# A scan over 25 chunks of nodes: passes ordered step by step, own rows added in PSUM, and the DMA transpose used from pass 12 on

## The chip, the core and the metric

The kernel runs on one core of a Trainium2 chip. The metric is the device time of one execution in microseconds (us). Three runs of the kernel before took 3808.49, 3808.58 and 3815.07 us; the median is 3808.58.

## The reference

Inputs are node features x (6250 nodes, 256 channels) and 206,250 edges sorted by destination. What is computed, cut to what matters:

```python
# 1. graph attention over layernorm(x)
h = (layernorm(x) @ W).reshape(n, 4, 64)
e = leaky_relu(a_src[src] + a_dst[dst], 0.2)
alpha = softmax of e over the edges of each destination
x = x + relu(segment_sum(alpha * h[src], dst) + bias)
# 2. a scan of 30 steps over layernorm(x), row by row
def step(h, _):
    h = h + 0.01 * tanh(h)
    h = h * sigmoid(h)
    h = layernorm(h) * ln_w + ln_b
    return einsum('bsc,dc->bsd', h, W) + b
x = x + scan(step, layernorm(x), length=30)
```

In the scan no row depends on another row, but each of a row's 30 steps depends on the one before it.

## The kernel before

**Tiles and chunks.** The nodes lie in 49 tiles of 128 rows x 256 channels, one row of each tile per partition. For the scan two tiles make a chunk (`CH = 2`), which gives `NC = 25` chunks; the last, chunk 24, has one tile. A *pass* is one scan step of one chunk, so there are 30 x 25 = 750 passes (`ALL`), numbered in the order of the list `ORDER`.

**Attention first.** Up to about 2200 us the core gathers edge rows and forms sums by destination. The scan's function `scan_ffn` then finishes the attention per tile: it fetches a tile's sum row (`end_row`, an indirect DMA from GpSimd), weights it (`gathered`, VectorE, `scale`), weights the tile's own row, the self loop (`own_tile`, four ScalarE instructions a tile, one for each head, `own`), adds the two (`own_added`, VectorE, `add`), adds the result to X behind a relu (`added`, VectorE, `both`), and takes the layernorm statistics (`spread`, `means`, `roots`) and the normalised rows (`normalise`, ScalarE, `ready`). For the first 14 tiles (7 chunks) this is done at once, the adding on TensorE (`add_own`). The other 35 tiles come in five batches of seven, and their pieces are laid between the passes: `PLANS` gives for each batch and stage the step at which it starts and every how many steps a tile follows. `due(q, stage)` says which piece stands at step q.

**One pass.** Each engine has its own instruction stream, written out step by step by a function `step(p)`. For pass q:

1. ScalarE `tanh(q)`: waits for the `affine` of the same chunk's previous pass (`act.wait_ge(s_aff, ...)`, line 1389).
2. GpSimd `add(q)`: h + tanh(h), line 1286.
3. ScalarE `silu(q)`, line 1369.
4. VectorE `stats(q)` (two instructions, one for each tile) and `moments(q)`; it waits for `silu(q)`, line 1579.
5. The transpose, in one of two ways. *Near*: four TensorE transposes into PSUM (`transposes`) and a ScalarE copy back (`copy_t`). *Far*: ScalarE splits each 32-bit word into two 16-bit halves (`split`, line 1381), SyncE sends them to DRAM (`send`, line 1216) and a transposing DMA brings them back (`turn`, line 1223). `FAR[q]` says which.
6. TensorE `product(q)`: four 32-bit products of 128x128 with 128x256, which the profile counts as eight matmuls, line 1682.
7. GpSimd `root(q)`: 1/sqrt of the variance; from `FAR0` on one instruction for three passes.
8. VectorE `affine(q)`: scales the product by the root and adds the bias, one instruction for each tile, line 1600. It frees the chunk for its next pass.

**The order of the steps.** Within step p ScalarE does `tanh(p)`, then `split(p-2)` if that pass is far, then `silu(p-1)`, then `copy_t(p-3)`. VectorE runs ahead (`AHEAD = 3`) and its affine behind (`BEHIND = 2`):

```python
lead = p.on(AHEAD)
lag = p if p.n < FAR0 else p.on(-BEHIND)
if leads: stats(lead)
if lags:  affine(lag, 0)
if leads: moments(lead)
if lags:  affine(lag, 1)
```

TensorE does `transposes(p)`, then `product(p-2)` before FAR0 and `product(p-4)` after it. SyncE does `send(p)`, then `turn(p-2)`. All streams are in order.

**Which chunks are in turn.** `ORDER` runs chunks 0 to 6 twelve times (84 passes, all near, `FAR0 = 84`), then chunks 0 to 9 eighteen times, chunks 10 to 16 and 7 to 9 twelve times, chunks 10 to 24 eighteen times, and chunks 17 to 24 twelve times. From pass 84 on chunks 0, 3, 6, ... are near and the others far: 432 passes of 750. Seventeen turns of the 15 chunks stand in a hardware loop on every engine (`iterate`); the rest is straight code.

Of the kernel before, what the change touches and what calls it, by code (L numbers as in the profile page):

```python
# [51 lines left out]
QT = 7  # L52
# [12 lines left out]
U = 5  # L65
assert NC % U == 0 and CH == 2 and SHORT == 1
# [8 lines left out]
assert len(ORDER) == ALL and len(LATER) % U == 0  # L75


FAR0 = JOIN * LAG
TURN = len(LATER)
RT, RX, RV, G3 = 3, 5, TURN, 3  # L80
assert TURN % RT == 0 and TURN % RX == 0 and TURN % G3 == 0 and FAR0 % G3 == 0 and ALL % G3 == 0
NEAR_J = [j for j in range(NC) if j % 3 == 0]
assert NC - 1 in NEAR_J
FAR = [q >= FAR0 and j not in NEAR_J for q, j in enumerate(ORDER)]
# [16 lines left out]
PASS = [q + 1 for q in range(ALL)]  # L101
# [5 lines left out]
XB = [0, 1, 2, 0, 1]  # L107
BANKED = []
for q in range(ALL):
    same = [p for p in range(max(q - 2 * TURN, 0), q) if not FAR[p] and XB[p % RX] == XB[q % RX]]  # L110
    BANKED.append(NEARS[same[-1]] if same else 0)

TOGETHER = ORDER.index(NC - 1) + 1
LOOPS = ITERS - LAG - 1
OUT = [0, JOIN, NA, NB, 20, 23, NC]
APART = TOGETHER + LOOPS * len(LATER)
assert all(ORDER[q] == LATER[(q - TOGETHER) % len(LATER)] for q in range(TOGETHER - len(LATER), APART))

SEEN = {}
FORMER = []  # L120
for q, j in enumerate(ORDER):
    FORMER.append(SEEN.get(j))
    SEEN[j] = q


FT = [0, 4, 8, 14, 21, 28, 35, 42, NT]
NF = len(FT) - 1
FRONT = 3
assert FT[FRONT] == CH * JOIN
OWN_ACT = [2, 2, 3]  # L130
assert all(b - a == QT for a, b in zip(FT[FRONT:], FT[FRONT + 1:]))


class Plan:


    def __init__(self, fetch, pace, below, share, norm, scale, own, add, step, mean, root, ready, every):
        n = QT
        self.at = dict(fetch=(fetch, pace, n), below=(below, 1, 1), share=(share, 1, 1), norm=(norm, 1, 1),
                       scale=(scale, step, n), own=(own, step, n), add=(add, step, n), both=(add + 1, step, n),  # L140
                       spread=(add + 2, step, n), mean=(mean, 1, 1), root=(root, 1, 1), ready=(ready, every, n))


AHEAD, BEHIND = 3, 2
DONE = {q0 + 3 * (j - j0) + BEHIND: j for j0, j1, q0 in ((0, JOIN, SEEN[0] + 5), (JOIN, NA, SEEN[JOIN] + 5), (NA, NB, APART + 2))
        for j in range(j0, j1)}
DONE.update({SEEN[j] + 2 + BEHIND: j for j in range(NB, NC)})


PLANS = {FRONT: Plan(5, 3, 25, 33, 34, 35, 42, 43, 4, 70, 77, 80, 2)}  # L150
for b in range(FRONT + 1, NF):
# [4 lines left out]
def due(q, stage):  # L156

    if q.r is not None:
        return None
    for b, plan in PLANS.items():  # L160
        first, every, count = plan.at[stage]
        i = q.n - first
        if 0 <= i < every * count and i % every == 0:
            return b, i // every
    return None
HS = 100.0


class At:


    def __init__(self, n, r=None):
        self.n, self.r, self.j, self.w = n, r, None, 0
        if 0 <= n < ALL:
            self.j = ORDER[n]
            self.w = SHORT if self.j == NC - 1 else CH
            self.u, self.v, self.t = n % RX, n % RV, n % RT
            self.far = FAR[n]

    def on(self, d):  # L180
        return At(self.n + d, self.r)

    def runs(self):
        return 0 <= self.n < ALL

    def of(self, table, less=0, times=1):

        n, rise = self.n, 0
        if self.r is not None:
            rise = table[n + TURN] - table[n]  # L190
            assert all(table[n + k * TURN] == table[n] + k * rise for k in range(LOOPS))
        first = times * (table[n] - less)
        return first if self.r is None or not rise else self.r * (times * rise) + first
# [936 lines left out]
def scan_ffn(nc, sem, res, dram, out, s_merged):  # L1130
# [3 lines left out]
    with ExitStack() as ctx:  # L1134
# [20 lines left out]
        assert U == 5 and FT[1] * C == 2 * 512 == (FT[2] - FT[1]) * C and (FT[3] - FT[2]) * C == 3 * 512  # L1155
# [9 lines left out]
        s_ownt = sem("s_ownt")  # L1165
        s_taken = sem("s_taken")
# [28 lines left out]
        def iterate(eng, step, after):  # L1195

            for q in range(TOGETHER):
                step(At(q))
            with eng.Fori(0, LOOPS) as r:
                for n in range(TOGETHER, TOGETHER + TURN):  # L1200
                    step(At(n, r))
            for q in range(APART, ALL + after):
                step(At(q))

        def sync(sp):
# [5 lines left out]
            def send(q):  # L1211
                sp.wait_ge(s_split, q.of(FARS))
                sp.nop(nofuse=True)
                wait_count(sp, s_turned[q.u], q.of(TURNED, 1, 16))
                sp.nop(nofuse=True)
                sp.dma_start(turned[q.u, :, :], hs[:, q.t, :].bitcast(U16)).then_inc(s_sent[q.t], 16)

            def turn(q):
                sp.wait_ge(s_sent[q.t], q.of(SENT, 0, 16))
                sp.nop(nofuse=True)  # L1220
                wait_count(sp, s_prod, q.of(PASS, RX))
                sp.nop(nofuse=True)
                sp.dma_start_transpose(h2T[:, q.u, :].bitcast(U16).rearrange("p (b n) -> p b n", n=2 * P),
                                       turned[q.u, :, :].rearrange("p (l c) -> (p l) c", l=2)).then_inc(s_turned[q.u], 16)
# [3 lines left out]
            def store(j0, j1):  # L1228
                sp.wait_ge(s_fin, j1)
# [9 lines left out]
            loads = {PLANS[b - 2].at["add"][0] + PLANS[b - 2].at["add"][1] * (QT - 1) + 4: b for b in range(FRONT + 2, NF)}  # L1239
            stores = {max(d for d, j in DONE.items() if j0 <= j < j1) + 4: (j0, j1) for j0, j1 in zip(OUT, OUT[1:])}  # L1240

            def step(p):
                if p.r is None and p.n in loads:
                    b = loads[p.n]
                    sp.wait_ge(s_taken, b - FRONT - 1)
                    own_rows(b)
                if p.r is None and p.n in stores:
                    store(*stores[p.n])
                if p.runs() and p.far:
# [5 lines left out]
            iterate(sp, step, 2 + 10)  # L1255
            assert max(stores) < ALL + 12
            sp.wait_ge(s_out, 16 * parts[0])

        def gpsimd(pool):
# [20 lines left out]

            def add(q):
                pool.wait_ge(s_tanh, q.of(PASS))
                wait_count(pool, s_silu, q.of(PASS, RT))
# [4 lines left out]
            def root(q, count):  # L1288
                last = q.on(count - 1)
                pool.wait_ge(s_ve, last.of(PASS))  # L1290
                wait_count(pool, s_aff, last.of(PASS, RV))
# [17 lines left out]
            def step(p):  # L1309
                if p.r is None and p.n < 5:  # L1310
# [5 lines left out]
                if p.runs():  # L1316
                    add(p)
                q = p.on(-3)
# [5 lines left out]
            iterate(pool, step, 3)  # L1324

        def scalar(act):
# [57 lines left out]
            def tanh(q):  # L1384
# [3 lines left out]
                else:  # L1388
                    act.wait_ge(s_aff, q.of(PASS, q.n - FORMER[q.n]))
                wait_count(act, s_add, q.of(PASS, RT))  # L1390
# [26 lines left out]
            def step(p):  # L1417
                if p.r is None and p.n < 5:
# [310 lines left out]
```

## Time and profile before

| | |
|---|---|
| median of 3 runs | 3808.58 us |
| profiled execution | 3808.91 us |
| its span, first to last instruction | 3807.1 us |
| TensorE, VectorE, ScalarE, GpSimd busy | 1542.5, 3081.4, 2453.4, 2987.5 us |
| GpSimd adds of the scan (line 1286) | 750, 941.0 us |
| product matmuls (line 1682) | 5880, 1348.1 us |
| transposing DMAs (line 1223) | 432, median 3.3 us from issue to landing |

The page gives busy times over the whole span, and in the slices of the span each digit is the busy share of one fortieth (95 us) in tenths. Since the attention stage fills more than half of the span, what the change touches has to be read in stretches behind 2237 us. Where instructions of an engine overlap (a ScalarE instruction of 0.62 us is followed after 0.52), the distance from start to start says what one costs, and not its duration.

### The profile page before, as it was taken

The page shows a single profiled execution, that of the slowest core. Times are in us where ns is not written, and L with a number is a line of the kernel's source. Part 1 is how long each engine was busy: PE and PEld are TensorE (multiplying, and loading weights), DVE is VectorE, ACT ScalarE, POOL GpSimd, SP SyncE. Part 2 cuts the span into 40 slices and gives each one's busy share as a digit, 9 for nine tenths or more (in the row PEclk, how much of TensorE's full clock was granted, in tenths as well). Part 3 has the DMA queues.
Part 4 walks back from the last instruction along what each step waited for, and adds up shares of the span by engine and source line. Part 5 has one row for each costly group of instructions (what it writes and reads, how often), then busy time and mean ns, then how long its engine had stood idle before and what let it go on. Part 6 is the DMA issues. An engine that isn't in the chain of part 4 may idle for free.

```text
span 3807.1 us, 42139 instructions
## 1 busy us (share of the span) xinstructions
PE 1542.5 (41%) x7470; PEld 1310.1 (34%) x7470; DVE 3081.4 (81%) x7292; ACT 2453.4 (64%) x3821; POOL 2987.5 (78%) x2856
## 2 busy tenths in 40 slices
PE   2400000000000000000000059999998999999988
PEld 2300000000000000000000048877876788888866
DVE  7477777877777878777877858989998988888877
ACT  4344444444444444444444557899999999999976
POOL 6777777777777777777777659988887889999876
PEclk8755555555555555555555569999999999999999
DMA  7366666666666666666666620266667777787766
GB/s 202 130 201 219 215 213 212 220 220 220 219 215 213 213 218 212 225 215 213 214 219 219 229 86 13 56 164 157 165 162 177 182 189 194 194 193 194 178 163 157
DMA packets 631730, 713.59 MB, mean 187 GB/s; under 512 B 499785, under 2 KB 501866, under 8 KB 615269
## 3 DMA queue, kind: packets, MB, share of 16 engines
q1 hardware_dynamic: 546180, 480.32, 42.4%
q0 software_dynamic: 83824, 230.16, 20.6%
q10 hardware_dynamic: 1536, 1.18, 0.2%
q14 instruction: 145, 1.19, 0.1%
q8 instruction: 45, 0.74, 0.1%
HBM read 249.79 MB, written 349.24 MB: 157 GB/s over the span
## 4 chain that ended last, share of the span: by engine, by line
POOL 40%; PE 21%; issue 19%; DMA 7%; ACT 6%; DVE 4%; SPq 0%; ACTq 0%; DVEq 0%; POOLq 0%
POOL G L737 36%; PE ps L1682 18%; DMA G<-haug,idx 3%; DMA h2T<-turned 3%; POOL h L1286 3%; ACT hs L1381 2%; PE ps L1668 2%; ACT h L1369 1%; ACT th L1392 1%; DVE cst L1582 1%; DVE Hs L1600 1%; POOL rs L1293 1%; PE psum L1016 1%; ACT own L1338 1%; DVE cmv L1591 1%
## 5 line engine op out<-in xcount | busy, mean ns | idle before, releaser
L737 POOL DMA_INDIRECT G<-haug,idx x1612 | 1524.4, 946 | 497.5 <-issue 482.8
L1682 PE MATMUL ps<-WT,h2T 128*128 128x256 f32 x5880 | 1348.1, 383 | 64.1 <-DMA h2T<-turned 61.7
L1682 PEld LDWEIGHTS ps<-WT,h2T 128*128 128x128 f32 x5880 | 1096.9, 191 | 226.4 <-DMA h2T<-turned 84.6
L1286 POOL TENSOR_TENSOR h<-Hs,th 128x512 f32<-128x512 f32 x750 | 941.0, 1265 | 188.5 <-ACT th L1392 179.5
L973 DVE TENSOR_TENSOR_SCAN RS<-keep,psum 128x845 f32<-128x845 f32 x496 | 940.2, 1898 | 0.2
L1058 PE MATMUL psum<-AD,ones 128*128 128x512 f32 x2 | 2.1, 1142 | 2052.5 <-DVE AD L1075 2052.5
L1600 DVE SCALAR_TENSOR_TENSOR Hs<-ps,rs,b 128x256 f32<-128x256 f32 x1470 | 675.4, 460 | 153.8 <-PE ps L1682 136.2
L644 ACT ACTIVATE G<-RS 128x845 f32<-128x845 f32 x496 | 782.2, 1723 | 26.6 <-DVE RS L973 25.5
L636 ACT ACTIVATE decay<-el,ZC 128x4 f32<-128x4 f32 x124 | 37.1, 299 | 1045.1 <-DVE el L943 1045.1
L1058 PEld LDWEIGHTS psum<-AD,ones 128*128 128x128 f32 x2 | 0.5, 310 | 2052.8 <-DVE AD L1075 2052.8
L1582 DVE BATCH_NORM_STATS2 cst<-h 128x6 f32<-128x256 f32 x1470 | 547.7, 413 | 51.9 <-ACT h L1369 49.7
L1369 ACT ACTIVATE h<-h 128x512 f32<-128x512 f32 x750 | 459.2, 612 | 65.6 <-POOL h L1286 62.6
L1392 ACT ACTIVATE th<-Hs 128x512 f32<-128x512 f32 x750 | 458.0, 611 | 42.9 <-DVE Hs L1600 38.7
L954 DVE TENSOR_TENSOR psum<-G,psum 128x845 f32<-128x845 f32 x496 | 477.5, 1031 | 2.4 <-ACT psum L637 2.4
L1381 ACT ACTIVATE hs<-h 128x1024 uint16<-128x1024 uint16 x432 | 451.2, 1044 | 10.2 <-DMA turned<-hs 10.2
L1293 POOL TENSOR_TENSOR rs<-cmv,half_neg 128x6 f32<-128x6 f32 (+1 forms) x306 | 360.0, 1177 | 26.9 <-DVE cmv L1591 25.7
L912 DVE TENSOR_TENSOR z<-G,AD 128x52 f32<-128x52 f32 x124 | 30.4, 245 | 410.6 <-DMA G<-haug,idx 358.6
L1668 PE MATMUL ps<-ident,h 128*128 128x128 f32 x1212 | 191.6, 280 | 41.0 <-ACT h L1369 38.9
L1591 DVE BATCH_NORM_AGGREGATE cmv<-cst 128x2 f32<-128x9 f32 x1470 | 188.9, 169 | 1.2
L1375 ACT ACTIVATE h2T<-ps 128x512 f32<-128x512 f32 (+1 forms) x318 | 177.4, 559 | 10.9 <-PE ps L1668 10.9
L1668 PEld LDWEIGHTS ps<-ident,h 128*128 128x128 f32 x1212 | 151.3, 144 | 89.7 <-ACT h L1369 54.7
L963 DVE SCALAR_TENSOR_TENSOR psum<-RS,decay,psum 128x65 f32<-128x65 f32 x492 | 124.6, 322 | 0.6 <-DVE z L912 0.4
(161 smaller groups left out, 1175.5 us busy)
## 6 DMA issues: line engine op xcount, KB each, us to landing
sums<-G SPq DMA_DIRECT2D x124, 1716.0 KB, 6.6
turned<-hs SPq DMA_DIRECT2D x432, 256.0 KB, 2.4
G<-haug,idx POOLq DMA_INDIRECT x1612, 2.8
h2T<-turned SPq DMA_TRANSPOSE x432, 3.3
haug<-G SPq DMA_DIRECT2D x7, 924.0 KB, 3.7
X<-x SPq DMA_DIRECT2D x7, 784.0 KB, 21.6
own<-haug SPq DMA_DIRECT2D x5, 924.0 KB, 4.8
adz<-G SPq DMA_DIRECT2D x4, 830.5 KB, 32.3
```

The costliest lines, as they stand in the source:

```text
L644: last = nc.scalar.activation(G[:, k % R, :, h * HR:(h + 1) * HR].rearrange("p t f -> p f t"), RS[:, k % 2, h, :, :], ACT.Copy)
L737: pool.indirect_dma_start(out=G[:, u, t, :], out_offset=None, in_=haug[:, :], in_offset=bass.IndirectOffsetOnAxis(ap=idx[:, i % 2, u * T + ...
L954: last = v.tensor_tensor(ps_m[:, h, :, :].rearrange("p f t -> p t f"), G[:, u, :, h * HR:(h + 1) * HR], w, ALU.mult)
L973: v.tensor_tensor_scan(RS[:, k % 2, h, :, :].rearrange("p f t -> p (f t)"), keep[:, k % 2, :, :].rearrange("p f t -> p (f t)"), ps_m[:, h, ...
L1286: g.tensor_tensor(h1[:, q.t, 0:n], chunk_rows(Hs, q.j, q.w), th[:, q.t, 0:n], ALU.add).then_inc(s_add, 1)
L1369: nc.scalar.activation(h2[:, q.u, 0:n], h1[:, q.t, 0:n], ACT.Silu, scale=1.0 / HS).then_inc(s_silu, 1)
L1381: nc.scalar.activation(hs[:, q.t, :].bitcast(U16).rearrange("p (l c) -> p l c", l=2), h2[:, q.u, :].bitcast(U16).rearrange("p (c l) -> p l ...
L1392: nc.scalar.activation(th[:, q.t, 0:n], chunk_rows(Hs, q.j, q.w), ACT.Tanh, scale=1.0 / HS).then_inc(s_tanh, 1)
L1582: last = v.bn_stats(cst[:, q.v, a, 0:6], h2[:, q.u, a * C:(a + 1) * C])
L1600: ins = v.scalar_tensor_tensor(out=Hs[:, q.j * CH + a, :], in0=ps_g[q.u][:, a * C:(a + 1) * C], scalar=rs[:, q.v, a:a + 1], in1=b100[:, :] ...
L1668: last = nc.tensor.transpose(ps_x[XB[q.u]][:, n * P:(n + 1) * P], h2[:, q.u, n * P:(n + 1) * P], ident[:, :])
L1682: last = nc.tensor.matmul(ps_g[q.u][:, a * C:(a + 1) * C], h2T[:, q.u, (a * 2 + k) * P:(a * 2 + k + 1) * P], WT[:, k, :], start=(k == 0), ...
```

## The change

Four things change together.

1. **The order of the passes.** `ORDER` is made by a rule: at each step, of the chunks that are ready and were last passed at least 7 (before step 94) or 10 steps ago, the one with most passes left is taken; chunks 0 to 9 count as if they had 8 fewer left. The batches follow each other every 80 steps instead of every 67. The hardware loop is gone, all 750 passes are straight code, and the `nop` instructions between SyncE's waits are dropped.
2. **Own rows.** `own_tile` moves from ScalarE (four instructions a tile) to GpSimd (one). The VectorE add of own rows goes; TensorE adds both rows in a PSUM bank (`add_tile`), from which VectorE's `added` reads. The near transposes keep two PSUM banks instead of three.
3. **Far passes** begin with pass 12 (`FAR0 = 12`) and are those with q % 3 != 2, except of chunk 24.
4. **SyncE** issues `turn` one step behind `send` and no longer two.

The steps of ScalarE and of VectorE within a pass, `AHEAD` and `BEHIND` stay. Chunks are stored in eight groups (`OUT`).

```diff
-LAG = 12
-JOIN, NA, NB = 7, 10, 17
-LATER = list(range(NA, NC))
-ORDER = (list(range(JOIN)) * LAG + list(range(NA)) * (ITERS - LAG) + (list(range(NA, NB)) + list(range(JOIN, NA))) * LAG
-         + LATER * (ITERS - LAG) + list(range(NB, NC)) * LAG)
-FAR0 = JOIN * LAG
-NEAR_J = [j for j in range(NC) if j % 3 == 0]
-FAR = [q >= FAR0 and j not in NEAR_J for q, j in enumerate(ORDER)]
...
-PLANS = {FRONT: Plan(5, 3, 25, 33, 34, 35, 42, 43, 4, 70, 77, 80, 2)}
+PLANS = {FRONT: Plan(5, 3, 25, 33, 34, 35, 41, 43, 43, 4, 70, 77, 80, 2)}
 for b in range(FRONT + 1, NF):
-    q = 24 + 67 * (b - FRONT - 1)
-    PLANS[b] = Plan(q, 8, q + 54, q + 62, q + 63, q + 64, q + 71, q + 72, 9, q + 130, q + 138, q + 141, 3)
+    q = 24 + 80 * (b - FRONT - 1)
+    PLANS[b] = Plan(q, 8, q + 54, q + 62, q + 63, q + 64, q + 70, q + 72, q + 72, 11, q + 141, q + 148, q + 151, 3)
...
+def ready_at(j):
+    t = min(CH * j + CH, NT) - 1
+    if t < FT[FRONT]:
+        return 0
+    b = (t - FT[FRONT]) // QT + FRONT
+    first, every, _ = PLANS[b].at["ready"]
+    return first + every * (t - FT[b]) + 1
+
+ALL = ITERS * NC
+FAR0, EARLY = 12, 94
+APART, WIDE = JOIN, 10
+FAVOUR = 8
+
+def passes():
+    left, last, made = [ITERS] * NC, [-ALL] * NC, []
+    for q in range(ALL):
+        apart = APART if q < EARLY else WIDE
+        free = [j for j in range(NC) if left[j] and ready_at(j) <= q and q - last[j] >= apart]
+        j = max(free, key=lambda j: (left[j] - FAVOUR * (j < WIDE), -last[j], -j))
+        made.append(j)
+        left[j] -= 1
+        last[j] = q
+    return made
+
+ORDER = passes()
+FAR = [q >= FAR0 and q % 3 != 2 and j != NC - 1 for q, j in enumerate(ORDER)]
+DONE = {q + BEHIND + 2: j for j, q in SEEN.items()}
+OUT = [(10, 14), (14, 17), (17, 21), (21, NC), (0, 4), (4, 7), (7, 9), (9, 10)]
...
-        ps_x = [psum[:, n * 512:(n + 1) * 512] for n in (4, 5, 6)]
+        ps_x = [psum[:, n * 512:(n + 1) * 512] for n in (4, 5)]
+        ps_m = psum[:, 6 * 512:6 * 512 + C]
...
-        def iterate(eng, step, after):
-            for q in range(TOGETHER):
-                step(At(q))
-            with eng.Fori(0, LOOPS) as r:
-                for n in range(TOGETHER, TOGETHER + TURN):
-                    step(At(n, r))
-            for q in range(APART, ALL + after):
-                step(At(q))
+        def iterate(step, after):
+            for q in range(ALL + after):
+                step(At(q))
...
 SyncE:
-            loads = {PLANS[b - 2].at["add"][0] + PLANS[b - 2].at["add"][1] * (QT - 1) + 4: b for b in range(FRONT + 2, NF)}
+            loads = {PLANS[b - 2].last("add") + 2: b for b in range(FRONT + 2, NF)}
+            stores = {max(SEEN[j] for j in range(j0, j1)) + BEHIND + 6: (j0, j1) for j0, j1 in OUT}
-                q = p.on(-2)
-                if q.runs() and q.far:
+                q = p.on(-1)
+                if q.runs and q.far:
                     turn(q)
...
 GpSimd:
+            def own_tile(b, i):
+                if i == 0:
+                    pool.wait_ge(s_own[b], 16)
+                    pool.wait_ge(s_part, b + 1)
+                o = own[:, b % 2, i, 0:SUMS].rearrange("p (h f) -> p h f", h=H)[:, :, 0:HID]
+                g.tensor_tensor(o, o, part[:, b % 2, 1, i, :].unsqueeze(2).to_broadcast([P, H, HID]), ALU.mult).then_inc(s_ownt, 1)
...
 ScalarE:
-                if due(p, "own"):
-                    own_tile(*due(p, "own")).then_inc(s_ownt, 1)
...
 VectorE:
-            def own_added(b, i0, i1):
-                hs = tile_heads(Hs[:, FT[b] + i0:FT[b] + i1, :], HID)
-                return v.tensor_tensor(hs, hs, tile_heads(own[:, b % 2, i0:i1, :], HR), ALU.add)
...
+                    gathered(b, i, i + 1).then_inc(s_weighted, 1)
                 if due(q, "both"):
                     b, i = due(q, "both")
+                    n = tiles_before(b) + i
+                    dve.wait_ge(s_joined, n + 1)
+                    added(b, i, i + 1, ps_m).then_inc(s_taken, 1)
...
 TensorE:
+            def add_tile(b, i):
+                n = tiles_before(b) + i
+                pe.wait_ge(s_weighted, n + 1)
+                pe.wait_ge(s_ownt, n + 1)
+                wait_count(pe, s_taken, n)
+                to = heads(ps_m, HID)
+                nc.tensor.matmul(to, ident[:, :], heads(Hs[:, FT[b] + i, :], HID), start=True, stop=False)
+                nc.tensor.matmul(to, ident[:, :], heads(own[:, b % 2, i, :], HR), start=False, stop=True).then_inc(s_joined, 1)
...
             def step(p):
+                if due(p, "add"):
+                    add_tile(*due(p, "add"))
                 if 4 <= p.n < ALL and not p.far:
                     transposes(p)
```

## Rows read from the trace of the kernel before

**Rows 1.** The page, busy tenths in 40 slices of the span

```profile
PE   2400000000000000000000059999998999999988
...
PEclk8755555555555555555555569999999999999999
```

**Rows 2.** Stretches, GpSimd's line 1286 alone: bounds, length, busy (count), clock, DMA share, GB/s

```profile
2279.00:2439.70 160.70, 92.01 (x72) 1.00 0.06 17
2463.20:2799.00 335.80, 198.45 (x156) 0.98 0.66 160
3017.60:3098.00 80.40, 50.92 (x40) 1.00 0.74 181
3632.80:3662.20 29.40, 12.20 (x10) 0.88 0.73 166
3683.40:3786.30 102.90, 58.60 (x49) 0.98 0.66 156
```

**Rows 3.** Stretches: PE, PEld, DVE, ACT, POOL busy (count), clock, DMA share, GB/s

```profile
2463.00:2862.20 399.20, 370.96 (x1789) 313.43 (x1789) 364.88 (x1230) 373.11 (x659) 343.02 (x274) 0.99 0.67 161
3158.40:3428.60 270.20, 270.20 (x1342) 237.67 (x1341) 241.19 (x870) 269.31 (x450) 247.13 (x201) 1.00 0.79 194
```

**Rows 4.** Timeline of TensorE in the hardware loop: start, length, instruction

```profile
3190.44 0.60 PE L1668 MATMUL ps<-ident,h 128*128 128x128 f32 x4
3190.87 5.35 PE L1682 MATMUL ps<-WT,h2T 128*128 128x256 f32 x24
```

**Rows 5.** Timeline of ScalarE in the hardware loop

```profile
3185.01 1.04 ACT L1381 ACTIVATE hs<-h 128x1024 uint16<-128x1024 uint16 x1
3185.96 0.61 ACT L1369 ACTIVATE h<-h 128x512 f32<-128x512 f32 x1
3186.48 0.57 ACT L1375 ACTIVATE h2T<-ps 128x512 f32<-128x512 f32 x1
3186.95 0.62 ACT L1392 ACTIVATE th<-Hs 128x512 f32<-128x512 f32 x1
```

**Rows 6.** Groups by line from 2463 to 2862 us: count, busy, mean ns, idle before

```profile
L1338 ACT ACTIVATE own<-own,partw 128x64 f32<-128x64 f32 x80 | 21.1, 339 | 0.0
...
L1493 DVE SCALAR_TENSOR_TENSOR X<-Hs,X 128x256 f32<-128x256 f32 x19 | 15.2, 803 | 0.0
L1489 DVE TENSOR_TENSOR Hs<-Hs,own 128x256 f32<-128x256 f32 x19 | 14.8, 781 | 0.0
...
L1345 ACT ACTIVATE Hs<-X,nmr,rstd 128x256 f32<-128x256 f32 x14 | 8.3, 591 | 0.0
...
L1369 ACT ACT_TABLE_LOAD x2 | 2.6, 1283 | 0.0
```

**Rows 7.** Timeline of ScalarE and VectorE in the stretch with 8 chunks

```profile
3708.75 0.61 ACT L1369 ACTIVATE h<-h 128x512 f32<-128x512 f32 x1
...
3709.39 0.75 DVE L1582 BATCH_NORM_STATS2 cst<-h 128x6 f32<-128x256 f32 x2 [0.27 <-ACT h L1369]
...
3710.06 0.47 DVE L1600 SCALAR_TENSOR_TENSOR Hs<-ps,rs,b 128x256 f32<-128x256 f32 x1
...
3711.18 0.63 ACT L1392 ACTIVATE th<-Hs 128x512 f32<-128x512 f32 x1 [0.51 <-DVE Hs L1600]
...
3711.72 1.04 ACT L1381 ACTIVATE hs<-h 128x1024 uint16<-128x1024 uint16 x1
...
3712.66 0.62 ACT L1369 ACTIVATE h<-h 128x512 f32<-128x512 f32 x1
```

**Rows 8.** Groups by line and shape in the hardware loop, 3158.4 to 3428.6 us

```profile
L1286 POOL TENSOR_TENSOR h<-Hs,th 128x256 f32<-128x256 f32 x10 | 7.3, 732 | 0.0
```

**Rows 9.** Waits, whole span: who waited for whom, total us, times, longest

```profile
PEld ps L1682 <- DMA h2T<-turned: 84.6, 81, 9.1
```

**Rows 10.** A stretch at half clock, all engines

```profile
2263.00:2273.00 10.00, 7.05 (x23) 5.46 (x24) 5.85 (x21) 6.95 (x13) 9.47 (x10) 0.50 0.10 27
```

**Rows 11.** Timeline of TensorE in that stretch

```profile
2269.06 3.62 PE L1682 MATMUL ps<-WT,h2T 128*128 128x256 f32 x8
2272.47 0.74 PE L1668 MATMUL ps<-ident,h 128*128 128x128 f32 x3
```

More of the change, by code:

```diff
@@ L82, with __init__, last @@
-NEAR_J = [j for j in range(NC) if j % 3 == 0]
-assert NC - 1 in NEAR_J
-FAR = [q >= FAR0 and j not in NEAR_J for q, j in enumerate(ORDER)]
+assert CH == 2 and SHORT == 1
+FT = [0, 4, 8, 14, 21, 28, 35, 42, NT]
+NF = len(FT) - 1
+FRONT = 3
+JOIN = FT[FRONT] // CH
+assert FT[FRONT] == CH * JOIN
+OWN_ACT = [2, 2, 3]
+assert all(b - a == QT for a, b in zip(FT[FRONT:], FT[FRONT + 1:]))
+HS = 100.0
+class Plan:
+    def __init__(self, fetch, pace, below, share, norm, scale, own, add, both, step, mean, root, ready, every):
+        n = QT
+        self.at = dict(fetch=(fetch, pace, n), below=(below, 1, 1), share=(share, 1, 1), norm=(norm, 1, 1),
+                       scale=(scale, step, n), own=(own, step, n), add=(add, step, n), both=(both, step, n),
+                       spread=(both + 1, step, n), mean=(mean, 1, 1), root=(root, 1, 1), ready=(ready, every, n))
+    def last(self, stage):
+        first, every, count = self.at[stage]
+        return first + every * (count - 1)
@@ new lines, with due @@
+PLANS = {FRONT: Plan(5, 3, 25, 33, 34, 35, 41, 43, 43, 4, 70, 77, 80, 2)}
+for b in range(FRONT + 1, NF):
+    q = 24 + 80 * (b - FRONT - 1)
+    PLANS[b] = Plan(q, 8, q + 54, q + 62, q + 63, q + 64, q + 70, q + 72, q + 72, 11, q + 141, q + 148, q + 151, 3)
+def due(q, stage):
+    for b, plan in PLANS.items():
+        first, every, count = plan.at[stage]
+        i = q.n - first
+        if 0 <= i < every * count and i % every == 0:
+            return b, i // every
+    return None
+def ready_at(j):
[5 more added lines that the diff above has]
+    return first + every * (t - FT[b]) + 1
@@ L87, in tally @@
+FORMER = []
+for q, j in enumerate(ORDER):
+    FORMER.append(SEEN.get(j))
+    SEEN[j] = q
+RT, RX, RV, G3 = 3, 5, 15, 3
+assert RV % G3 == 0 and FAR0 % G3 == 0 and ALL % G3 == 0
+FAR = [q >= FAR0 and q % 3 != 2 and j != NC - 1 for q, j in enumerate(ORDER)]
 def tally(marks):
@@ L98, in ring_tally @@
     return of
-PASS = [q + 1 for q in range(ALL)]
 NEARS = tally(not f for f in FAR)
@@ L106 @@
 ROOTS = [q + 1 if q < FAR0 else FAR0 + (q - FAR0) // G3 + 1 for q in range(ALL)]
[L107 to L141, printed above, removed]
@@ L166, with __init__ @@
-HS = 100.0
-class At:
[L172 to L175, printed above, removed]
+AHEAD, BEHIND = 3, 2
+DONE = {q + BEHIND + 2: j for j, q in SEEN.items()}
+FINISHED = {DONE[d]: n + 1 for n, d in enumerate(sorted(DONE))}
+OUT = [(10, 14), (14, 17), (17, 21), (21, NC), (0, 4), (4, 7), (7, 9), (9, 10)]
+assert sorted(j for a, b in OUT for j in range(a, b)) == list(range(NC))
+class At:
+    def __init__(self, n):
+        self.n = n
+        self.runs = 0 <= n < ALL
+        if self.runs:
+            self.j, self.far = ORDER[n], FAR[n]
@@ L176, in __init__ @@
             self.w = SHORT if self.j == NC - 1 else CH
-            self.u, self.v, self.t = n % RX, n % RV, n % RT
-            self.far = FAR[n]
+            self.u, self.v, self.t, self.x = n % RX, n % RV, n % RT, NEARS[n] % 2
     def on(self, d):
[L181 to L193, printed above, removed]
+        return At(self.n + d)
@@ L1228, in store @@
             def store(j0, j1):
-                sp.wait_ge(s_fin, j1)
+                sp.wait_ge(s_fin, max(FINISHED[j] for j in range(j0, j1)))
                 for p0, p1, t0, t1, rows in node_rows(out, j0 * CH, min(j1 * CH, NT)):
@@ L1238, in sync @@
                 own_rows(b)
-            loads = {PLANS[b - 2].at["add"][0] + PLANS[b - 2].at["add"][1] * (QT - 1) + 4: b for b in range(FRONT + 2, NF)}
-            stores = {max(d for d, j in DONE.items() if j0 <= j < j1) + 4: (j0, j1) for j0, j1 in zip(OUT, OUT[1:])}
+            loads = {PLANS[b - 2].last("add") + 2: b for b in range(FRONT + 2, NF)}
+            stores = {max(SEEN[j] for j in range(j0, j1)) + BEHIND + 6: (j0, j1) for j0, j1 in OUT}
+            assert len(stores) == len(OUT)
             def step(p):
-                if p.r is None and p.n in loads:
+                if p.n in loads:
                     b = loads[p.n]
-                    sp.wait_ge(s_taken, b - FRONT - 1)
+                    sp.wait_ge(s_joined, tiles_before(b - 1))
                     own_rows(b)
-                if p.r is None and p.n in stores:
+                if p.n in stores:
                     store(*stores[p.n])
-                if p.runs() and p.far:
+                if p.runs and p.far:
                     send(p)
-                q = p.on(-2)
-                if q.runs() and q.far:
+                q = p.on(-1)
+                if q.runs and q.far:
                     turn(q)
-            iterate(sp, step, 2 + 10)
-            assert max(stores) < ALL + 12
+            iterate(step, BEHIND + 7)
             sp.wait_ge(s_out, 16 * parts[0])
@@ L1288, in root @@
             def root(q, count):
[L1289 to L1291 removed]
+                last = q.n + count - 1
+                pool.wait_ge(s_ve, last + 1)
+                wait_count(pool, s_aff, last + 1 - RV)
                 of = slice(q.v, q.v + count)
@@ L1309, in step @@
             def step(p):
-                if p.r is None and p.n < 5:
+                if p.n < 5:
                     return
@@ L1315, in step @@
                     roots(due(p, "root")[0])
-                if p.runs():
+                if p.runs:
                     add(p)
+                if due(p, "own"):
+                    own_tile(*due(p, "own"))
                 q = p.on(-3)
@@ L1322, in step @@
                     root(q.on(1 - G3), G3)
-            iterate(pool, step, 3)
+            iterate(step, 3)
         def scalar(act):
@@ L1417, in step @@
             def step(p):
-                if p.r is None and p.n < 5:
+                if p.n < 5:
                     return
@@ L1421, in step @@
                     shares(due(p, "share")[0])
-                if due(p, "own"):
-                    own_tile(*due(p, "own")).then_inc(s_ownt, 1)
                 if due(p, "ready"):
                     normalise(*due(p, "ready"))
-                if p.runs():
+                if p.runs:
                     tanh(p)
                 q = p.on(-2)
-                if q.runs() and q.far:
+                if q.runs and q.far:
                     split(q)
                 q = p.on(-1)
-                if q.runs():
+                if q.runs:
                     silu(q)
@@ L1436, in step @@
                     copy_t(q)
-            iterate(act, step, 3)
+            iterate(step, 3)
         def vector(dve):
@@ L1642, in step @@
                     affine(lag, 1)
-                if p.r is None and p.n in DONE:
+                if p.n in DONE:
                     final(DONE[p.n])
-            iterate(dve, step, BEHIND + 2)
+            iterate(step, BEHIND + 2)
         def tensor(pe):
@@ L1704, in step @@
                     product(p.on(-4))
-            iterate(pe, step, 4)
+            iterate(step, 4)
         return sync, gpsimd, scalar, vector, tensor
```

134 lines of the change are left out of this document (45 added, 89 removed).

## The prediction, made before the kernel was run

> **What bounds the kernel now.** The page's slices come first: up to the 23rd an attention stage runs, in which TensorE is nearly idle and which the change does not touch. From 2237 us on the scan runs: 750 passes (30 steps of 25 chunks), each with one GpSimd add, so the adds counted in a stretch give its pace [rows 1, 2]. I divide: 160.7/72 = 2.23 us a pass in the start phase (7 chunks in turn, all transposed on TensorE), 335.8/156 = 2.15 with 10 chunks in turn, 80.4/40 = 2.01 where these have hardly any work beside them, 102.9/49 = 2.10 with the last 8. The hardware loop, 15 chunks in turn, took 270.2 us for 150 passes (GpSimd's 201 are 150 adds, 50 roots and one that reaches in): 1.80 [rows 3].
>
> What a pass takes of an engine is the distance from one start to the next. TensorE: 0.43 for four transposes [rows 4]; its loop turn is 27.02 us with 4.5 chunks transposed and 14.5 multiplied, so a product takes (27.02 - 1.94)/14.5 = 1.73. ScalarE: split 0.95, silu 0.52, copy 0.47, tanh 0.52 like silu [rows 5]. The loop is TensorE's: busy 270.2 of 270.2 [rows 3]. With 10 chunks nobody is full: TensorE needs 1.73 + 0.4 x 0.43 = 1.90 a pass; ScalarE 1.04 + 0.6 x 0.95 + 0.4 x 0.47 + (21.1 + 8.3 + 2 x 2.6)/187 = 1.98, the bracket being own rows, normalising and two kinds of table loads, one of them shown [rows 6]; VectorE 364.9/187 = 1.95; GpSimd 343.0/187 = 1.83 [rows 3]. The 2.15 lies 0.17 over the largest; the 2.01 lies 0.15 over 1.73 + 0.3 x 0.43 = 1.86.
>
> **The order written out by hand.** What each stage waits for is in the code, its price in the trace. VectorE's step p is stats(p+3), then affine(p) before FAR0 and affine(p-2) from FAR0 on. ScalarE's step p is tanh(p), split(p-2), silu(p-1), copy. tanh(p) waits for the affine of its chunk's previous pass, with 7 chunks affine(p-7). Before, this stood in VectorE's step p-7, behind stats(p-4): slack of three steps. Now FAR0 goes from 84 to 12 while the chunks in turn stay 7, so affine(p-7) stands in step p-5, **behind stats(p-2)**, which waits for silu(p-2), which ScalarE issues in step p-1, the last thing of weight ahead of tanh(p). So silu(p-2), stats(p-2), affine(p-7), tanh(p), split(p-2), silu(p-1) is a closed ring that holds one pass; nothing overlaps round it. The last stretch of before, with 8 chunks, has the same ring with two passes in it and shows the links: silu starts at 3708.75, stats 3709.39, affine (two halves) 3710.06, tanh 3711.18, split 3711.72, the next silu 3712.66 [rows 7]. Once round is 3.91 us, and 0.94 less, 2.97, for a pass without a split. Two of three passes are split: (2 x 3.91 + 2.97)/3 = 3.60 a pass. With 8 chunks the ring allows 1.95, under the 2.10 measured; there the way through the DMAs, 8 x 2.10 = 16.8 us, decides.
>
> **The change part by part.** The new order, worked out from the rule in the diff, has distance 7 for passes 19 to 82 and once at 90, and 10 or more from 94 on; 472 passes are split (432 before), 278 transposed on TensorE.
> - Passes 0 to 11: unchanged, pass 12 starts at 2279.0 [rows 2].
> - Passes 12 to 18 and 83 to 93: 18 at the 2.23 of before or a little more, 2.3: 41.
> - Passes 19 to 82: 64 x 3.60 = 230, plus 3 for one exp table change (1.28 there and 1.28 back [rows 6]), which stands in the ring: 233. They took 143. VectorE's tile pieces (the longest 0.80 [rows 6]) fit its idle part of a round, 3.60 less the 1.79 from stats to tanh [rows 7], and GpSimd's new work fits too: nothing. If that cover failed, 7 tiles with three pieces of at most 0.80 would be 17.
> - Passes 94 to 433: own rows leave ScalarE (0.26 x 80 = 21.1 of 187 passes) and the own add leaves VectorE (14.8) [rows 6]. GpSimd gets 7 multiplies in 80 passes: 0.73 each as its 128x256 add [rows 8], at most the 1.27 of a 128x512 one. TensorE gets two matmuls a tile: half a product, 0.86. Tile work comes every 80 passes, not every 67. Per pass: TensorE 1.73 + 0.14 + 0.08 = 1.95; ScalarE 1.04 + 0.63 + 0.16 + 0.08 = 1.91; GpSimd 1.83 + 0.06 = 1.89 (1.94 with 1.27); VectorE 1.95 - 0.11 = 1.84. add_tile puts three waits on TensorE, and transposes and products, and behind these the affines, queue behind them; but the weighting is 8 steps earlier, the own multiply 2, the previous tile's taking 11: none is last. On this floor comes 0 to 0.17, as before. SyncE issues the transposing DMA one step, some 2 us, earlier, and waits for it were in the list [rows 9], so I take 0.10: 340 x 2.05 = 697.
> - Passes 434 to 679: no tile work, one short chunk in 10, 3.4 transposed: (9.5 x 1.73 + 3.4 x 0.43)/10 = 1.79. The hardware loop is gone and the distance is 10, not 15; that costs 0 to 0.15 (the 2.01 stretch, straight code with 10 chunks). Between the two, 0.08: 246 x 1.87 = 460.
> - Passes 680 to 749: floor 1.84, plus 0.10: 136. The store of 14 tiles made 10 passes last 29.4 us, 8.4 over 21.0 [rows 2]; 22 tiles leave between steps 684 and 695 and 7 at 732, by size 17; the longer distance covers a part: 14. Sum 150.
> - At nothing: SyncE's dropped nops; the third PSUM bank for transposes (two now hold six passes' worth); the fetches of own rows, still three later ones; the 25 closing adds on VectorE, at two tiles each about 25 x 1.6 = 40 us in 70 passes at the most, which fill VectorE without passing TensorE's 1.84 by more than the 0.10 taken.
> - Tail: 3807.1 - 3786.3 = 20.8. 20 tiles instead of 15 are stored after the last turn, 0.66 MB at the stretch's 156 GB/s [rows 2], 4 us, half of it under the last products: 23.
>
> Sum: 2279 + 41 + 233 + 697 + 460 + 150 + 23 = 3883 of span. The profiled execution took 1.8 more than its span (3808.9 to 3807.1; the median is 3808.6): **3885 us**, 2.0% slower. Up to pass 84 the sum gives 251 us where 161 stood; from there to the last add 1330 where 1347 stood.
>
> A rule of the Trainium skill (TensorE: Matmul & The Clock Gate, Part 1) speaks further against the change: half clock is the resting state, and only activity releases it. The trace agrees: with TensorE busy 7.05 of 10 us the granted clock was 0.50, its lower level [rows 10].
>
> **Rivals.**
> 1. The ring does not close, and the 7 chunks are held only by the way through the DMAs: 16.8 less the one step of 2.1 is 14.7, over 7 is 2.10, so 64 x 1.50 = 96 less: 3789, faster. For: rows 7 show a round with time to spare, and no stretch of before has a ring of one pass. Against: each link is a step of an in-order engine or a semaphore in the code. It decides if passes 19 to 82 run under 2.3. 10%.
> 2. The ring at half clock: a product then took 2272.47 - 2269.06 = 3.41 [rows 11], a third of the transposes twice 0.14 more: 3.70 a pass, over the 3.60, so TensorE becomes the bound: 64 x 0.10 = 6 more, 3891. For: TensorE would be busy 1.87 of 3.60, less than in rows 10. Against: the gaps are short, and over the start phase the clock held 1.00 [rows 2]. 15%.
> 3. The ring as priced, the later passes at their floors, the stores free: 34 + 20 + 14 less, 3817. Against: no straight stretch of before stood at its floor. 10%.
> 4. The ring, and later passes with the old excess: 340 x 0.07 + 246 x 0.07 = 41 more, 3926. For: the distance stays 10 to the end. 15%.
>
> **How the numbers follow.** The forecast (3850 to 3910) has 50%. Only rival 1 is faster; this kernel's measurement tells 0.2%, 7.6 us, from no change. Faster 0.09, within 0.03, slower 0.88. The range leaves out rival 1 and part of 3: 3830 to 3930.
>
> **What would show it.** Right: adds of passes 19 to 82 about 3.6 us apart, there VectorE idle ahead of stats with silu as the releaser and ScalarE idle ahead of tanh with affine as the releaser, once a pass; 2.05 for passes 94 to 433, 1.87 for 434 to 679; own multiplies near 0.73. Wrong: a start phase that stays at some 2.2 us a pass.

## The result, and the profile after

The changed kernel took 3859.67 us (median of 4 runs, 3855.04 to 3863.41). Its ratio to the kernel before, from the means of four runs each, is 1.0129, 95% interval [1.0111, 1.0147]: slower, as forecast, by 1.3% where 2.0% was said, and inside the range. The profiled execution took 3855.04 us with a span of 3853.2.

The page of the changed kernel, as in [rows 1]; the scan's first slices, the 24th to 26th, are where TensorE is less busy than behind and its clock low:

```profile
PE   2400000000000000000000066789999999999998
...
PEclk8755555555555555555555578899999999999999
```

The stretches of the changed kernel by the adds of its passes (now line 1288), as in [rows 2]: passes 19 to 83, 94 to 433, 434 to 679, 680 to 748. A count one above the passes is an add that reaches in.

```profile
2295.50:2538.00 242.50, 82.42 (x66) 0.82 0.42 103
...
2564.10:3244.30 680.20, 432.21 (x341) 1.00 0.77 183
3244.40:3687.30 442.90, 297.86 (x246) 1.00 0.71 176
3687.40:3830.90 143.50, 86.14 (x70) 0.98 0.74 181
```

242.5/65 = 3.73 us a pass in the start phase, which was 2.23 [rows 2]; 680.2/340 = 2.00 where 2.15 stood for the first 156 of these passes and 2.11 for all 340 (716.7 us from add to add); 442.9/246 = 1.80, as in the old hardware loop [rows 3], which was 1.84 over the same 246 passes (452.8 us); 143.5/69 = 2.08. Pass 94 starts 101 us later than before, and the way from there to the last add is 56 us shorter: 1266.9 where it was 1323.4.

The same stretches with all instructions of the changed kernel, columns as in [rows 3]:

```profile
2295.50:2538.00 242.50, 166.35 (x630) 136.09 (x629) 119.25 (x430) 130.00 (x202) 125.90 (x106) 0.82 0.42 103
...
2564.10:3244.30 680.20, 669.53 (x3284) 578.94 (x3283) 609.20 (x2187) 651.77 (x1057) 621.47 (x511) 1.00 0.77 183
```

In the start phase VectorE, ScalarE and GpSimd are busy about half of the time, TensorE 69% of it at a lowered clock, and nothing is full; in passes 94 to 433 TensorE nearly is, 669.5 of 680.2, with ScalarE close behind, 651.8. The waits of the start phase (2295 to 2538 us: who waited for whom, total us, times, longest) are near-equal, about one each per pass, which is how a closed ring looks:

```profile
POOL h L1288 <- ACT th L1396: 116.1, 61, 4.1
DVE cst L1555 <- ACT h L1373: 115.0, 64, 3.8
ACT th L1396 <- DVE Hs L1573: 114.4, 63, 2.8
...
DVE Hs L1573 <- PE ps L1663: 8.8, 15, 0.9
```

One round of it in the timeline, the same links as [rows 7], but now with every pass in its own round:

```profile
2357.36 0.62 ACT L1373 ACTIVATE h<-h 128x512 f32<-128x512 f32 x1
...
2358.00 0.75 DVE L1555 BATCH_NORM_STATS2 cst<-h 128x6 f32<-128x256 f32 x2 [2.25 <-ACT h L1373]
...
2358.67 0.47 DVE L1573 SCALAR_TENSOR_TENSOR Hs<-ps,rs,b 128x256 f32<-128x256 f32 x1
...
2359.78 0.63 ACT L1396 ACTIVATE th<-Hs 128x512 f32<-128x512 f32 x1 [1.33 <-DVE Hs L1573]
...
2360.32 1.04 ACT L1385 ACTIVATE hs<-h 128x1024 uint16<-128x1024 uint16 x1
...
2361.27 0.61 ACT L1373 ACTIVATE h<-h 128x512 f32<-128x512 f32 x1
```

From silu to silu 3.91 us, to the hundredth what rows 7 gave; VectorE idles 2.25 of it waiting for silu, ScalarE 1.33 waiting for affine.

### The profile page after: what moved, and what is told of

The parts are those of the page before. It is cut to its first block, busy times and chain, and to the rows that moved or that the text cites. A ratio compares the mean times of both kernels' runs of the same rounds, so it can differ in the third digit from the quotient of the medians.

```text
span 3853.2 us, 38727 instructions
## 1 busy us (share of the span) xinstructions
PE 1571.7 (41%) x7450; PEld 1341.9 (35%) x7450; DVE 3035.4 (79%) x7257; ACT 2435.4 (63%) x3681; POOL 2988.6 (78%) x2843
## 4 chain that ended last, share of the span: by engine, by line
POOL 38%; PE 22%; issue 18%; DMA 9%; ACT 5%; DVE 4%; SPq 2%; ACTq 0%; DVEq 0%; POOLq 0%
POOL G L732 36%; PE ps L1663 18%; DMA turned<-hs 4%; DMA G<-haug,idx 3%; ACT hs L1385 2%; PE ps L1649 2%; DMA h2T<-turned 2%; SPq L1216 2%; POOL h L1288 2%; ACT h L1373 1%; DVE Hs L1573 1%; ACT th L1396 1%; PE psum L1011 1%; DVE cst L1555 1%; DVE cmv L1564 1%
## 5 line engine op out<-in xcount | busy, mean ns | idle before, releaser
L1663 PE MATMUL ps<-WT,h2T 128*128 128x256 f32 x5880 | 1365.9, 387 | 25.6 <-DMA h2T<-turned 24.2
L1663 PEld LDWEIGHTS ps<-WT,h2T 128*128 128x128 f32 x5880 | 1118.0, 195 | 190.8 <-DMA h2T<-turned 44.7
L1288 POOL TENSOR_TENSOR h<-Hs,th 128x512 f32<-128x512 f32 (+1 forms) x750 | 936.9, 1260 | 250.6 <-ACT th L1396 245.3
L1555 DVE BATCH_NORM_STATS2 cst<-h 128x6 f32<-128x256 f32 x1470 | 547.7, 413 | 156.4 <-ACT h L1373 155.2
L1396 ACT ACTIVATE th<-Hs 128x512 f32<-128x512 f32 (+1 forms) x750 | 458.5, 612 | 116.9 <-DVE Hs L1573 116.9
L1385 ACT ACTIVATE hs<-h 128x1024 uint16<-128x1024 uint16 x472 | 493.7, 1046 | 17.9 <-DMA turned<-hs 17.1
L1373 ACT ACTIVATE h<-h 128x512 f32<-128x512 f32 (+1 forms) x750 | 458.6, 611 | 45.4 <-POOL h L1288 44.9
L1295 POOL TENSOR_TENSOR rs<-cmv,half_neg 128x6 f32<-128x6 f32 (+1 forms) x258 | 339.9, 1318 | 13.7 <-DVE cmv L1564 12.8
L1649 PE MATMUL ps<-ident,h 128*128 128x128 f32 x1052 | 171.3, 286 | 96.7 <-ACT h L1373 95.8
L1649 PEld LDWEIGHTS ps<-ident,h 128*128 128x128 f32 x1052 | 135.4, 147 | 136.1 <-ACT h L1373 104.6
L1379 ACT ACTIVATE h2T<-ps 128x512 f32<-128x512 f32 (+1 forms) x278 | 154.7, 557 | 13.6 <-PE ps L1649 13.5
```

The costliest lines, as they stand in the source:

```text
L1288: g.tensor_tensor(h1[:, q.t, 0:n], chunk_rows(Hs, q.j, q.w), th[:, q.t, 0:n], ALU.add).then_inc(s_add, 1)
L1385: nc.scalar.activation(hs[:, q.t, :].bitcast(U16).rearrange("p (l c) -> p l c", l=2), h2[:, q.u, :].bitcast(U16).rearrange("p (c l) -> p l ...
L1396: nc.scalar.activation(th[:, q.t, 0:n], chunk_rows(Hs, q.j, q.w), ACT.Tanh, scale=1.0 / HS).then_inc(s_tanh, 1)
L1555: last = v.bn_stats(cst[:, q.v, a, 0:6], h2[:, q.u, a * C:(a + 1) * C])
L1649: last = nc.tensor.transpose(ps_x[q.x][:, n * P:(n + 1) * P], h2[:, q.u, n * P:(n + 1) * P], ident[:, :])
L1663: last = nc.tensor.matmul(ps_g[q.u][:, a * C:(a + 1) * C], h2T[:, q.u, (a * 2 + k) * P:(a * 2 + k + 1) * P], WT[:, k, :], start=(k == 0), ...
```

## The experiments

Ratios are to the kernel before, measured beside each experiment: its median was 3806.3 us beside experiments 1 to 4, 3811.5 beside 5, 6, 7 and 10, and 3811.8 beside 8 and 9. So ratios, and not microseconds, are compared between these groups. The paces are from one profiled execution of each kernel.

**1. FAR0 back at 84** (`FAR0, EARLY = 84, 94`), all else as changed.

> The changed kernel with FAR0 back at 84: no far passes and no lagging affine in the start phase; everything else as changed. Passes 19 to 83 took 3.73 us each against 2.23 before. If the whole loss sits in the start phase, they return to 2.23 (up to 2.35, as only two PSUM banks are left for near transposes) and the time is 3860 - 65 x 1.45 = 3766, with the paces behind pass 94 unchanged at 2.00 and 1.80. If the new order and the own rows cost time elsewhere, it stays over 3800.

Measured 3755.67 us, ratio 0.9860 [0.9843, 0.9877]. Its stretches for passes 19 to 83, 94 to 433 and 434 to 679, line 1288 alone:

```profile
2296.30:2446.50 150.20, 82.80 (x65) 1.00 0.05 16
2471.00:3151.00 680.00, 431.64 (x340) 1.00 0.74 183
3151.10:3595.50 444.40, 297.78 (x246) 1.00 0.71 176
```

2.31 a pass at the start, and 2.00 and 1.81 behind it unchanged. The profiled spans of this and the changed kernel differ by 93.7 us, 92.3 of them in passes 19 to 83: the whole loss sits in the start phase. Without it the rest of the change is worth 1.4%: **this version beats both kernels**, and no other experiment beat it. The 0.08 a pass over the old 2.23 are 5 us. The own rows are not their cause, for the start phase still took 2.31 a pass with the multiply put back on ScalarE (experiment 5) and 2.35 with the add put back on VectorE (experiment 9); the missing third bank is a candidate that no run tested.

**2. The affine ahead of stats**, far passes kept from 12 on.

```diff
                 lags = p.n < FAR0 or FAR0 <= lag.n < ALL
+                if FAR0 <= p.n < EARLY:
+                    if lags:
+                        affine(lag, 0)
+                        affine(lag, 1)
+                    stats(lead)
+                    moments(lead)
+                    return
                 if leads:
                     stats(lead)
```

> The changed kernel with far passes from 12 on, but in steps 12 to 93 VectorE does both affines ahead of stats and moments. Ring theory: the affine of the chunk's previous pass no longer stands behind the newest stats, so the ring of one pass opens; what is left is a ring through TensorE (silu, near transposes, three products, affine, tanh, silu) of some 7.2 us per 3 passes, so 2.4 us a pass, time 3860 - 65 x 1.33 = 3774. Rival, the way through the DMAs holds the 7 chunks: the start phase stays at 3.7 whatever VectorE's order, time 3860.

Measured 3797.68 us, 0.9978 [0.9968, 0.9988]: a change of order alone, not one instruction fewer, and 1.5% of time against the changed kernel. Passes 19 to 83:

```profile
2291.00:2475.20 184.20, 83.76 (x65) 0.94 0.54 136
```

The start phase went from 3.73 to 184.2/65 = 2.83. So the rival (the DMAs hold the 7 chunks at 3.7) is out, but my 2.4 was too low. The waits of this kernel in passes 19 to 83 (transposes are line 1656, products 1670):

```profile
ACT th L1396 <- DVE Hs L1573: 53.3, 33, 4.5
...
PE ps L1656 <- ACT h L1373: 41.3, 21, 5.2
DVE Hs L1573 <- PE ps L1670: 31.9, 26, 3.4
```

This fits the second ring, through TensorE: 21 near transposes, one per three passes, wait 2 us each for the newest silu, and affine waits 31.9 us for the products behind them, where it waited 8.8 in the changed kernel. Experiment 7 tests it.

**3. Near passes with the late affine**: `FAR = [q >= 84 and ...]` with `FAR0 = 12`, so the start phase has no split and no transposing DMA, and only the order that hangs on FAR0: the later affine, the later product, and one root for three passes.

> The changed kernel with FAR0 = 12 for the lags, but all passes up to 83 near: no split, no DMA in the start phase, only the late affine (and late product). Ring theory: a round without a split, 2.96 us a pass, or somewhat more where TensorE's transposes and products at half clock come late; time 3860 - 65 x 0.75 = 3811. Rival, the DMAs are what costs: the start phase falls to 2.23 and the time to 3762.

One run, 3805.45 us (span 3803.6). Passes 19 to 83:

```profile
2296.00:2488.40 192.40, 82.45 (x65) 1.00 0.04 12
```

192.4/65 = 2.96 a pass, the round without a split that rows 7 gave (2.97), at clock 1.00 and with the DMAs nearly idle (share 0.04). The lags alone, without any DMA transpose, cost 0.65 a pass against experiment 1, which differs from this kernel only in them. Of the three it is the later affine: up to pass 83 VectorE waited for nothing but silu, no affine for a product or a root. All its waits from 2295 to 2487 us:

```profile
DVE cst L1555 <- ACT h L1373: 75.3, 64, 2.8
```

With experiment 2, which moves only VectorE's order, this shows the ring.

**4. Turn two steps behind send again** (`p.on(-2)` in SyncE's step).

> The changed kernel with SyncE's turn two steps behind send again. Behind pass 94 the changed kernel is TensorE-bound at 2.00 and 1.80 us a pass. If the earlier turn is what lets 10 chunks in turn run at TensorE's pace, the paces go back towards 2.12 and 1.95, 70 us more, 3930; if it is the new order and the lighter ScalarE and VectorE, they stay and the time is within 10 us of 3860.

Measured 3852.27 us, 1.0116 [1.0099, 1.0133], not to be told from the changed kernel; passes 94 to 433 at 2.00. The earlier turn is worth nothing here.

**5. Own rows multiplied on ScalarE again**, from experiment 1: the call of `own_tile` moves from GpSimd's step back into ScalarE's.

> The changed kernel with FAR0 = 84, and the multiplies of own rows back on ScalarE (four per tile) instead of GpSimd. Passes 94 to 433 ran at 2.00 us each with TensorE busy nearly all the time. If TensorE is the bound there (floor 1.95), 1.05 us more on ScalarE per tile, 0.09 a pass, brings ScalarE only to 2.00 and the time stays within 10 us of 3756. If the lighter ScalarE is what made 2.15 into 2.00, the pace goes to about 2.08 and the time to 3756 + 340 x 0.08 = 3783.

Measured 3775.99 us, 0.9906 [0.9889, 0.9922], 0.5% over experiment 1. All engines in passes 94 to 433, first this kernel, then experiment 1:

```profile
2471.20:3164.90 693.70, 671.63 (x3280) 579.16 (x3280) 609.02 (x2183) 674.40 (x1165) 604.95 (x482) 1.00 0.75 179
```

```profile
2471.00:3151.00 680.00, 668.48 (x3286) 579.13 (x3285) 608.58 (x2187) 651.53 (x1057) 621.74 (x510) 1.00 0.74 183
```

13.7 us more, with ScalarE busy 22.9 more. That lies between the two expected values, under 10 and 27. TensorE was not the only bound: its work did not change and the stretch grew. With ScalarE at 674 and TensorE at 672 of 694 both are nearly full; that each waits for the other now and then is my reading, which no run tested.

**6. The kernel before with `FAR0 = 12` alone.**

> The kernel before with one edit: FAR0 = 12, so four of seven passes are far from 12 on and the affine lags. Ring theory: rounds of 3.91 with and 2.96 without a split, (4 x 3.91 + 3 x 2.96)/7 = 3.50 a pass for 65 passes instead of 2.23, and about 0.1 more for TensorE at half clock: 3806 + 65 x 1.35 = 3894. Rival, the loss of the changed kernel comes from its order of passes or its own rows and not from FAR0: 3806 or less.

One run, 3917.85 us beside 3811.5. Passes 19 to 83:

```profile
2296.80:2535.20 238.40, 82.45 (x65) 0.83 0.37 91
```

238.4/65 = 3.67 a pass (3.50 plus 0.1 was said). The early far passes alone, on the old order and the old own rows, cost 2.8%, as much as they cost in the changed kernel (1.0129 against 0.9860); the other parts have no share in the loss.

**7. Product ahead of the near transposes too**, on top of experiment 2 (TensorE, steps 16 to 93).

> The changed kernel with both affines ahead of stats in steps 12 to 93 (this alone gave 2.84 us a pass there) and also TensorE's product(p-4) ahead of transposes(p) in steps 16 to 93. If what was left is the ring through TensorE, where the products of three passes queue behind near transposes that wait for the newest silu, it opens: 2.2 us a pass, 3798 - 65 x 0.6 = 3759. If the way through the DMAs or the half clock holds the 7 chunks now, it stays near 2.8 and 3798.

Measured 3775.30 us, 0.9907 [0.9891, 0.9924]. Passes 19 to 83:

```profile
2295.50:2457.20 161.70, 84.40 (x66) 0.98 0.61 154
```

161.7/65 = 2.49 a pass. The second ring opened (2.83 to 2.49), the 2.2 was missed. Waits of passes 19 to 83:

```profile
PEld ps L1670 <- DMA h2T<-turned: 28.6, 27, 5.6
ACT th L1396 <- DVE Hs L1573: 20.7, 24, 4.3
PE ps L1670 <- DMA h2T<-turned: 18.0, 17, 5.2
```

Now the DMAs are waited for, and tanh waits less for affine, 20.7 us after 53.3 in experiment 2. From the start of tanh to the end of affine a far pass of passes 20 to 79 took 16.7 us in the median, worked out from the timeline, which over 7 chunks is 2.39. That is no proof of a third limit: with 7 chunks in turn this way lasts nearly 7 passes whatever holds them, and a near pass took 16.5.

**8. Only one pass of three far before pass 84**, from experiment 7.

> The kernel with both orders turned round in the start phase (affines ahead of stats, product ahead of transposes; 2.49 us a pass with two of three passes far), but with only one of three passes far before pass 84. If the way through the DMAs is what holds the 7 chunks there (16.7 us from tanh to affine, over 7 is 2.39), two near passes of three shorten it and the pace goes to 2.1, 3775 - 65 x 0.4 = 3749, below the 2.31 that all-near passes took. If TensorE's near transposes hold it, it stays at 2.4 or more, 3770.

Measured 3768.83 us, 0.9886 [0.9870, 0.9903]. Passes 19 to 83:

```profile
2295.20:2450.40 155.20, 83.85 (x65) 0.99 0.35 89
```

155.2/65 = 2.39 a pass. A miss: less than with two of three far, but not 2.1, and still over the 2.31 of all near. TensorE's waits for the DMA fell from 18.0 to 6.5 us and those of tanh for affine stood at 29.0; which chain holds it then I did not resolve.

**9. Own rows added on VectorE again**, from experiment 1: `own_added` in place of `add_tile`, and `added` reads the sum from SBUF, one step later.

> The changed kernel with FAR0 = 84, and own rows added on VectorE again (0.76 us a tile, and the relu add then reads SBUF instead of PSUM, 0.79 instead of 0.41) and not on TensorE (0.86 us a tile less there). VectorE takes 1.1 us more a tile, 0.10 a pass. If TensorE's load is what bounds passes 94 to 433 at 2.00, they get 0.08 faster, 3756 - 340 x 0.07 = 3732. If the lighter VectorE is what brought the pace from 2.15 to 2.00, they get slower, 2.05 and 3773.

Measured 3769.55 us, 0.9892 [0.9870, 0.9914], over experiment 1, with intervals that just overlap. Passes 94 to 433, columns as in experiment 5:

```profile
2469.20:3154.20 685.00, 657.86 (x3177) 556.91 (x3176) 637.43 (x2215) 652.19 (x1057) 624.40 (x510) 1.00 0.76 182
```

685.0/340 = 2.01 a pass. TensorE had some 24 us less to do, estimated from 28 tiles at 0.86 us, and was busy 10.6 us less; VectorE was busy 28.9 us more. Nothing got faster, so TensorE's load by itself is not what a pass waits for last. As the run shifts work between two engines, it does not price either alone.

**10. The kernel before with every third pass near** from 84 on.

> The kernel before with one edit: from pass 84 on every third pass is near (and chunk 24), as in the changed kernel, instead of the chunks 0, 3, 6 and so on. With 10 chunks in turn 3.3 instead of 4 passes of ten are near, which lowers TensorE's floor by 0.03 and raises ScalarE's by 0.03. If the even spacing of near passes is what brings 2.15 down to 2.00 behind pass 94, the time falls by 170 to 290 passes x 0.12, to about 3780; if that came from the own rows, it stays within 8 us of 3806.

Measured 3800.14 us, 0.9971 [0.9959, 0.9982]. Passes 94 to 349, first this kernel, then the kernel before:

```profile
2462.80:3004.30 541.50, 329.06 (x256) 0.99 0.74 178
```

```profile
2463.20:3017.60 554.40, 328.30 (x256) 0.98 0.69 167
```

That is 2.12 and 2.17 a pass. Even spacing together with fewer near passes (3.3 instead of 4 of ten) is a small part of the gain; the run does not part the two.

## Why the prediction was right, point by point

| term, us | forecast | changed kernel |
|---|---|---|
| to the start of pass 94 | 2279 + 41 + 233 = 2553 | 2564 |
| passes 94 to 433 | 697 | 680 |
| passes 434 to 679 | 460 | 443 |
| passes 680 to the last add | 150 | 144 |
| tail | 23 | 22 |
| span | 3883 | 3853.2 |

**The ring** was right in place, links and price. Experiment 2 moved only VectorE's order and took 0.9 off a pass; experiment 3 left only the lags and gave 2.96; experiment 6 brought the loss into the kernel before by one number. In the changed kernel's timeline the distances from silu to silu of passes 19 to 80 are 3.91, 3.91 and 2.96 in turn, to within 0.02, save for the round with the exp table (1.5 more, where 3 was forecast), one that was 0.28 longer, and the rounds behind a near pass. Rival 1, an open ring held by the DMAs, is refuted: with both orders turned round, and as many far passes, the 7 chunks ran at 2.49 (experiment 7), so the way through the DMAs alone holds them at no more than that.

**Half clock (rival 2)** came about in part, on top of the ring. In the ring TensorE stood idle up to 5.32 us at a time, the granted clock went back and forth between its two levels, 0.82 in the mean of the stretch, and three products took 6.94 us at a mean clock of 0.77, where [rows 4] has 5.35:

```profile
2350.31 1.12 PE L1649 MATMUL ps<-ident,h 128*128 128x128 f32 x4 [5.32 <-ACT h L1373]
2351.22 6.94 PE L1663 MATMUL ps<-WT,h2T 128*128 128x256 f32 x24
```

The affines then waited 8.8 us for products in all, and the rounds behind near passes were up to 0.98 us longer than the ring, 10.3 us in all. That 65 x (3.73 - 3.60) is 8.5 is in part luck, since the last three rounds, as the ring opened, were 4.8 us shorter. The size of 6 given to that rival was near, its mechanism was not: TensorE did not become the bound, busy 166 of 242.5 us, but delayed up to one round in three. The gaps that I called short were not. No run held the clock up in this ring, so the price rests on the trace; that experiment 3, at clock 1.00, stood at its 2.96 speaks for it.

**The later passes** were mis-sized. From pass 94 to the last add 16 us less than before was forecast (1307 for 1323), and 56 came: an excess of 0.10 and 0.08 a pass was put over the floors of 1.95 and 1.79, and 0.05 and 0.01 came. That is 34 us too much; with 7 from the last two terms, and 11 too little up to pass 94, it makes the 30 by which the span was missed: errors of opposite sign, which partly cancelled. Two reasons that I gave fell: the earlier turn (experiment 4: nothing) and a price for straight code with distance 10 instead of the hardware loop with 15 (1.80 in both). And "TensorE's floor plus something" was too simple a picture of passes 94 to 433: moving load from TensorE to VectorE gained nothing (experiment 9), giving 1.05 us a tile to ScalarE cost 14 us (experiment 5).

**Where the 56 us from pass 94 on come from.** By stretch, 36.5 came in passes 94 to 433, 10 in 434 to 679 and 10 behind these. By part, 13 go with the new choice of near passes in passes 94 to 349 (experiment 10, in the old order), 14 with the multiply off ScalarE (experiment 5), 5 with the add off VectorE in passes 94 to 433 (experiment 9; 685.0 against 680.0, one profile each). These were measured on different kernels and need not add up. The rest, about 24, I did not take apart; open are the end, where the distance is 10 and no longer 8 (2.23 to 2.08, 10 us), and the smaller stores.

## What to carry to other kernels

When streams are written out by hand, follow one item round all in-order engines and count the steps between a wait and what releases it: a lag that is free with 10 items in turn closed the ring with 7, and made a phase 67% slower in which no engine was full. The price of a ring can be read beforehand, as here, from a stretch that has the same links with more items in it. A lag and a feature that share one switch (here FAR0) should be tried apart.

## What the runs showed of the hardware

VectorE's relu add of a tile took 0.79 us in the mean with both inputs in SBUF and 0.41 with one of them in PSUM (groups by line and shape, passes 94 and later; the kernel before, then the changed one):

```profile
L1493 DVE SCALAR_TENSOR_TENSOR X<-Hs,X 128x256 f32<-128x256 f32 x28 | 22.2, 794 | 0.0
L1489 DVE TENSOR_TENSOR Hs<-Hs,own 128x256 f32<-128x256 f32 x28 | 21.3, 760 | 0.0
```

```profile
L1281 POOL TENSOR_TENSOR own<-own,partw 128x256 f32<-128x256 f32 x28 | 17.2, 613 | 0.0
...
L1491 DVE SCALAR_TENSOR_TENSOR X<-ps,X 128x256 f32<-128x256 f32 x28 | 11.6, 415 | 0.0
```

The form with both inputs in SBUF ran from 0.41 to 1.50 us with a median of 0.42, so it is not slow in itself but sometimes held up. Laid beside GpSimd's timeline, the ten of the 28 that took 1.23 us or more each overlapped one of GpSimd's adds of the scan (line 1286); of the other 18, at 0.41 to 0.49, only six did. Of the 28 with one input in PSUM 21 overlapped such an add, and all took 0.41 to 0.42. The Trainium skill (GPSIMD Engine Reference, 8. Key points) says that GpSimd shares its SBUF interfaces with VectorE and contends with VectorE instructions that have two SBUF inputs; these times agree. Over the 28 tiles adding in PSUM took the 21.3 us of the own add off VectorE and another 10.6 off the relu add that stays (22.2 to 11.6).

GpSimd's multiply with a broadcast operand took 0.61 us (L1281), where 0.73 was forecast from its add of the same shape [rows 8].
